# Relation sums from an always-one column and eight small DMAs, the 113-row transfers cut at a multiple of 16, and a later check of places, in a graph layer on one core

## What is computed

```python
h = maximum(layernorm(x), 0)
xs = h[src]
for r in range(4):
    w_r = where(edge_type == r, edge_weight, 0)
    total_msg += (xs @ W_rel[r] + b_rel[r]) * w_r[:, None]
agg = segment_sum(total_msg, dst) / maximum(segment_sum(edge_weight, dst), 1)[:, None]
x1  = layer_norm(h + h @ W_self + b_self + agg) * g1 + b1
ffn = gelu(x1 @ W_ffn1 + b_ffn1) @ W_ffn2 + b_ffn2
out = x + layer_norm(x1 + ffn) * g2 + b2
```

## Time and profile before

| | us |
|---|---|
| median of 3 runs (lowest, highest) | 349.38 (349.29, 350.85) |
| the profiled execution, its own time | 350.59 |
| its span, first to last instruction | 348.8 |
| busy: PE, PEld | 280.4, 250.1 |
| busy: DVE, ACT, POOL | 268.3, 144.9, 90.7 |
| mean granted TensorE clock | 0.949 |

### The profile page before, as it was taken

One profiled execution on the slowest core, in us unless ns is written; L12 is line 12 of the kernel. 1 busy time (PEld: TensorE's weight loads), 2 busy tenths in 40 slices (PEclk: granted clock), 3 DMA queues, 4 the chain that ended last, 5 costly groups with the idle time before them and its releaser, 6 DMA issues.

```text
span 348.8 us, 6519 instructions
## 1 busy us (share of the span) xinstructions
PE 280.4 (80%) x2602; PEld 250.1 (72%) x2602; DVE 268.3 (77%) x520; ACT 144.9 (42%) x180; POOL 90.7 (26%) x85
## 2 busy tenths in 40 slices
PE   2202965852999999999999999999999995999910
PEld 2201844642998899879997899879996895988810
DVE  4169999899979797979999798978434289796630
ACT  3033952735545456653745456553713224300000
POOL 3047392185000060001200040002100193493310
PEclk9999996995799999999999999999999998999985
DMA  5912114030000000000000000004006036001000
GB/s 164 265 28 59 63 26 155 2 121 3 2 0 2 3 3 2 2 1 2 2 3 2 0 3 2 3 0 166 18 2 210 31 106 181 14 0 60 30 34 23
DMA packets 8661, 15.62 MB, mean 45 GB/s; under 512 B 1667, under 2 KB 1887, under 8 KB 8630
## 3 DMA queue, kind: packets, MB, share of 16 engines
q1 hardware_dynamic: 8498, 15.03, 13.7%
q10 hardware_dynamic: 132, 0.17, 0.2%
HBM read 13.91 MB, written 1.28 MB: 44 GB/s over the span
## 4 chain that ended last, share of the span: by engine, by line
PE 54%; DVE 25%; issue 6%; DMA 4%; ACT 2%; POOL 2%; DVEq 2%; SPq 1%; POOLq 0%; ACTq 0%
PE psG L947 20%; PE psX L947 20%; PE psA L947 14%; DVE onehot L695 8%; DMA h<-in_x 4%; DVE wkey L697 3%; DVE keq L688 2%; DVE u_lo L924 2%; DVEq L624 1%; DVE u_hi L922 1%; ACT AT_hi L540 1%; POOL tbuf L343 1%; DVE A L713 1%; DVE small L752 1%; DVE tbuf L749 1%
## 5 line engine op out<-in xcount | busy, mean ns | idle before, releaser
L695 DVE TENSOR_SCALAR onehot<-iota_src,slot 125x640 f16<-125x640 f16 x200 | 77.1, 449 | 0.0
L947 PE MATMUL psA<-wkey,onehot 125*128 125x48 f16 (+5 forms) x1200 | 46.1, 196 | 18.0 <-DVE wkey L697 18.0
L947 PEld LDWEIGHTS psA<-wkey,onehot 125*128 125x128 f16 x1200 | 43.4, 99 | 21.9 <-DVE wkey L697 19.3
L505 ACT ACTIVATE away<-iota_src,slot 125x640 f16<-125x640 f16 x40 | 33.1, 827 | 40.4 <-PE psA L947 19.6
L947 PE MATMUL psG<-AT_hi,h_hi 128*128 128x256 f32 (+1 forms) x180 | 46.6, 295 | 0.4 <-ACT AT_hi L540 0.4
L947 PE MATMUL psG<-AT_hi,h_lo 128*128 128x256 f32 (+1 forms) x180 | 45.0, 286 | 0.0
L339 POOL TENSOR_SCALAR small<-small 128x1 f32<-128x1 f32 (+1 forms) x5 | 1.7, 333 | 165.3 <-DVE small L754 165.3
L947 PEld LDWEIGHTS psG<-AT_hi,h_hi 128*128 128x128 f32 (+1 forms) x180 | 34.8, 193 | 0.6 <-issue 0.5
L947 PEld LDWEIGHTS psG<-AT_hi,h_lo 128*128 128x128 f32 (+1 forms) x180 | 35.0, 194 | 0.0
L508 ACT ACTIVATE onehot<-away,ones_r 125x640 f16<-125x640 f16 x40 | 33.2, 829 | 1.3
L697 DVE TENSOR_TENSOR wkey<-keq,slot 125x624 f16<-125x624 f16 x40 | 32.9, 823 | 0.0
(11 more groups left out here) (154 smaller groups left out, 588.8 us busy)
## 6 DMA issues: line engine op xcount, KB each, us to landing
stage<-in_L_gnn_W_rel SPq DMA_DIRECT2D x8, 512.0 KB, 3.7
stage<-in_L_gnn_W_ffn SPq DMA_DIRECT2D x8, 512.0 KB, 4.1
h<-in_x SPq DMA_DIRECT2D x4, 256.0 KB, 4.2
stage<-in_L_gnn_W_self SPq DMA_DIRECT2D x2, 512.0 KB, 13.8
x_again<-in_x SPq DMA_DIRECT2D x4, 256.0 KB
out<-ybuf SPq DMA_DIRECT2D x4, 256.0 KB, 2.0
g_bc<-in_L_gnn_ln_g SPq DMA_DIRECT2D x2, 256.0 KB
b_bc<-in_L_gnn_ln_b SPq DMA_DIRECT2D x2, 256.0 KB
```

Of the source, the lines that this page charges most:

```text
L505: a.activation(away[0:EK, :], iota_src[0:EK, :], ACT.Abs, scale=-1.0, bias=slot[0:EK, b % SB, 0, SL - 1:SL]).then_inc(away_in, 1)
L695: v.tensor_scalar(oh[0:EK, j, :], iota_src[0:EK, :], f[:, 0, j:j + 1], None, ALU.is_equal)
L947: return nc.tensor.matmul(o, l, r, start=start, stop=stop, skip_group_check=True)
```

## The change

1. Transfers of a chunk of rows (load of x, second load of x, store of the result) are cut at a multiple of 16 rows: the chunk of 113 rows goes as 112 rows and 1 row.
2. The one-hot matrices are written 626 wide (OW), and column 626 holds a one for good. Row 114 of the last chunk of AT (SUMS) is then the column sum. `degrees` and evac_D are gone; SP moves that row of AT_hi and of AT_lo with 8 DMAs for each q (64 elements each, one relation to one partition) into D8 (8 x 128, two buffers), and b_rel is loaded twice, so that the bias product has 8 rows.
3. The check of places runs after the first build on DVE and after the first block on PE, and POOL takes the low part of W_self after the shift of the layer norm is out.

```diff
+    SPREAD = 16
+    SPANS = [[(0, m)] if m % SPREAD == 0 else [(0, m - m % SPREAD), (m - m % SPREAD, m)] for m in ROWS]
+    OW = N + 1
+    OS = OW + 1
+    SUMS = OS - 1 - (NT - 1) * P
...
             for c in range(NT):
-                sp.dma_start(h32[0:ROWS[c], c, :], x[c * P:c * P + ROWS[c], :]).then_inc(x_in[c], 16)
+                for p0, p1 in SPANS[c]:
+                    sp.dma_start(h32[p0:p1, c, :], x[c * P + p0:c * P + p1, :]).then_inc(x_in[c], 16)
+            def sums_by_relation(q):
+                if q >= 4:
+                    sp.wait_ge(W_ps, q // 2 - 1)
+                sp.wait_ge(AT_a, q + 1)
+                sp.wait_ge(AT_b, q + 1)
+                with nc.allow_non_contiguous_dma("one row to one partition by relation"):
+                    for part, half in enumerate((AT_hi, AT_lo)):
+                        row = f32(half[SUMS:SUMS + 1, q % 2, NT - 1, :]).rearrange("p (d r) -> p r d", r=R)
+                        for r in range(R):
+                            k = part * R + r
+                            sp.dma_start(D8[k:k + 1, q // 2 % 2, q % 2 * HD:(q % 2 + 1) * HD],
+                                         row[:, r, :]).then_inc(D_in[q % 2], 16)
+
             for u in range(NU):
+                if u == U_REL:
+                    for q in range(NQ - 2):
+                        sums_by_relation(q)
+                if u == U_REL + 2:
+                    for q in range(NQ - 2, NQ):
+                        sums_by_relation(q)
...
             g.tensor_tensor(rstd, var_e, mhalf, ALU.pow).then_inc(xrstd, 1)
+            pool.wait_ge(xnmr, 1)
             low_part(pool, 0)
...
-                    v.tensor_scalar(oh[0:EK, j, :], iota_src[0:EK, :], f[:, 0, j:j + 1], None, ALU.is_equal)
+                    v.tensor_scalar(oh[0:EK, j, 0:OW], iota_src[0:EK, 0:OW], f[:, 0, j:j + 1], None, ALU.is_equal)
...
-            def evac_D(q):
...
+            self_low(0)
+            low_part(dve, 1)
+            dve.wait_ge(iotas, 1)
+            dve.wait_ge(turned, 2)
+            pick(0, r[0])
+            build(0)
+            self_low(1)
 
             dve.wait_ge(first_in, 2)
...
-            self_low(0)
-            low_part(dve, 1)
-            dve.wait_ge(iotas, 1)
-            dve.wait_ge(turned, 2)
-            pick(0, r[0])
-            build(0)
...
-            def degrees(q):
...
             def rel_product(c):
 
                 m = ROWS[c]
-                pe.wait_ge(D_ev, 2 * c + 2)
-                mm(psX[0:m, :], D4[:, 0:m], brel_sb[:, :], True)
+                if c >= 1:
+                    pe.wait_ge(xT_b, c)
+                for i in range(2):
+                    pe.wait_ge(D_in[i], 16 * 2 * R * (c + 1))
+                mm(psX[0:m, :], D8[:, c % 2, 0:m], brel_sb[:, :], True)
...
-            pe.wait_ge(viol, 1)
-            pe.wait_ge(turned, 2)
-            mm(psA[:, NT - 1, 0:1], ones[0:EP, :], vsum, True, True).then_inc(vcnt, 1)
             self_product(0)
-            pe.wait_ge(regs_in, 1)
-            flag = pe.value_load(f_i32[0:1, NB:NB + 1], min_val=0, max_val=1 << 20)
             for i in range(HB):
                 build(0, range(i, i + 1))
+                if i == 0:
+                    pe.wait_ge(viol, 1)
+                    pe.wait_ge(hT_b, 2)
+                    mm(psG[:, 0, 0:1], ones[0:EP, :], vsum, True, True).then_inc(vcnt, 1)
+                    pe.wait_ge(regs_in, 1)
+                    flag = pe.value_load(f_i32[0:1, NB:NB + 1], min_val=0, max_val=1 << 20)
```

More of the change, by code:

```diff
@@ L40, in gnn_layer @@
     ROWS = [min(P, N - c * P) for c in range(NT)]
+    SPREAD = 16
+    SPANS = [[(0, m)] if m % SPREAD == 0 else [(0, m - m % SPREAD), (m - m % SPREAD, m)] for m in ROWS]
+    LOADED = [16 * len(spans) for spans in SPANS]
     EK = N // 5
@@ L63, in gnn_layer @@
     UC = 1024
+    OW = N + 1
+    OS = OW + 1
+    SUMS = OS - 1 - (NT - 1) * P
+    assert OW % 2 == 0 and OS <= NP
     EARLY = 3
@@ L217, in gnn_layer @@
         away_in = sem("away_in")
+        third = sem("third")
         keq_in = sem("keq_in")
@@ L228, in gnn_layer @@
         AT_b = sem("AT_b")
-        D_m = sem("D_m")
         G_ps = sem("G_ps")
@@ L232, in gnn_layer @@
         G_b = sem("G_b")
-        D_ps = sem("D_ps")
-        D_ev = sem("D_ev")
+        D_in = [sem(f"D_in{i}") for i in range(2)]
         deg_ps = sem("deg_ps")
@@ L370, in _ @@
                         sp.dma_start(buf[:, :], row.broadcast_to([P, D])).then_inc(consts_in, 16)
-                    sp.dma_start(brel_sb[:, :], b_rel).then_inc(consts_in, 16)
+                    for part in range(2):
+                        sp.dma_start(brel_sb[part * R:(part + 1) * R, :], b_rel).then_inc(consts_in, 16)
                     with nc.allow_non_contiguous_dma("bias by partition"):
@@ L381, in _ @@
             for c in range(NT):
-                sp.dma_start(x_again[0:ROWS[c], c, :], x[c * P:c * P + ROWS[c], :]).then_inc(late_in, 16)
+                for p0, p1 in SPANS[c]:
+                    sp.dma_start(x_again[p0:p1, c, :], x[c * P + p0:c * P + p1, :]).then_inc(late_in, 16)
             for buf, v in ((g2_bc, ln2_g), (b2_bc, ln2_b), (bf2_bc, b2)):
@@ L386, in _ @@
                 sp.wait_ge(y_out, c + 1)
-                sp.dma_start(out[c * P:c * P + ROWS[c], :], ybuf[0:ROWS[c], c % 2, :]).then_inc(out_done[c % 2], 16)
+                for p0, p1 in SPANS[c]:
+                    sp.dma_start(out[c * P + p0:c * P + p1, :], ybuf[p0:p1, c % 2, :]).then_inc(out_done[c % 2], 16)
             for i in range(2):
-                sp.wait_ge(out_done[i], 16 * len(range(i, NT, 2)))
+                sp.wait_ge(out_done[i], sum(LOADED[c] for c in range(i, NT, 2)))
         @block.gpsimd
@@ L440, in _ @@
                 low_part(pool, u)
-            pool.wait_ge(late_in, 16 * (NT + 3))
+            pool.wait_ge(late_in, sum(LOADED) + 16 * 3)
             for c in range(NT):
@@ L693, in build @@
                 oh, wk = ring(b)
+                if b == LATE + 2:
+                    v.memset(oh[0:EK, :, OW:NP], 0.0).then_inc(third, 1)
+                    dve.wait_ge(third, 1)
+                    v.memset(oh[0:EK, :, OS - 1:OS], 1.0)
                 for j in range(SL - 1):
-                    v.tensor_scalar(oh[0:EK, j, :], iota_src[0:EK, :], f[:, 0, j:j + 1], None, ALU.is_equal)
+                    v.tensor_scalar(oh[0:EK, j, 0:OW], iota_src[0:EK, 0:OW], f[:, 0, j:j + 1], None, ALU.is_equal)
                 dve.wait_ge(keq_in, b + 1)
@@ L1083, in rel_product @@
                 pe.wait_ge(G_b, 4 * c + 4)
-                mm(psG[0:m, 0, 0:1], D4[:, 0:m], ones[0:R, 0:1], True, True).then_inc(deg_ps, 1)
+                mm(psG[0:m, 0, 0:1], D8[:, c % 2, 0:m], ones[0:2 * R, 0:1], True, True).then_inc(deg_ps, 1)
                 for r in range(R):
```

29 lines of the change are left out of this document (13 added, 16 removed).

## The result

The changed kernel takes 332.27 us (median of 4 runs, 330.13 to 335.61) against 350.12 for the kernel before (4 runs, 349.29 to 351.39): the ratio is 0.947, interval 0.941 to 0.953. It is faster, as forecast, but by 18 us and not by 28, and it lies 2.3 us above the range. Medians and ranges in this document are of all runs, while the ratios leave out two (335.61 here and 353.81 of e3) that fell into a slower state of the chip.

What follows compares the result with a forecast made beforehand. The prediction took DVE to set the pace early and PE later. Start -9.8, four pairs -9.9, last pair +0.9 and end -8.9 summed to -27.7 us, from 349.38 to 322 us (rounded), range 316 to 330.

Steps and rivals of the forecast that it cites:

- the check of the eight DMAs: Steady pairs: issues 3.0 us plus landing 2.0, together 5.0, hidden in 7.75 us between AT_lo and the bias product.
- if rel_product waits for D8: Sign of being wrong: the bias product waits for the DMAs of the sums; the forecast expected no such wait.
- Four pairs, -9.9: Steady pairs: removing `degrees` takes 2.48 us a pair from PE, which is full there; four pairs give -9.9 us.
- Rival 3: Sums land late in the pairs: beyond 7.75 us each further us costs PE one us a pair; 328 or 367 us, chance 0.06.
- The last pair, +0.9: Last pair: the sums issued ahead of W_ffn1's third tile delay PE's early FFN product; gains nothing, loses 0.9 us.
- The start, -9.8: Start: fifth chunk's statistics 7.8 us earlier, layer norm's shift 2.0 us shorter, moved check 0; together -9.8 us.
- The end, -8.9: End: the last store, cut at 112 rows, takes 2.4 us against 11.3; -8.9 us.
- Rival 1: Start: W_self still lands late, so h starts 3.7 us earlier instead of 9.8; 328 us, chance 0.12.
- Rival 2: Order of the start or SP's queue (unit 12 late) costs 2 to 4 us more; 325 to 327 us, chance 0.15.
- Rival 5: More is gained, as the earlier check frees PE or unit 12 is hidden; 318 to 320 us, chance 0.08.
- Rival 4: DVE's one-hots of 626 columns lose their pace, 0.42 us more 200 times; 391 us, chance 0.04.

Runs made afterwards that it cites:

- e3: The kernel before with only the sums moved by DMA in place of the ones product: 350.37 us, ratio 0.999.
- e6: The changed kernel with the bias product behind the products of G high instead of ahead of them: 326.08 us, ratio 0.930.
- e7: The changed kernel with both e5's and e6's edits: 320.13 us, ratio 0.911.
- e8: The changed kernel with the four DMAs of AT_hi issued a second time, to rows that nothing reads: 348.95 us, ratio 0.994.
- e5: The changed kernel with unit 12 of the weights (third W_ffn1 tile) issued ahead of the last sums (q = 8 and 9): 324.76 us, ratio 0.924.
- e11: The changed kernel with each copy of sums reading 64 neighbouring elements in place of every fourth: 332.60 us, ratio 0.947.
- e1: The kernel before with only the transfers cut at 112 rows: 332.66 us, ratio 0.946.
- e2: The kernel before with only the later check of places and POOL's wait for the shift: 349.23 us, ratio 0.996.

## Why the prediction was wrong

**The step that failed** is the check of the eight DMAs: "Eight issues at 0.33 us, with 0.04 between them ... are 3.0 us". It was mis-sized: 0.59 us each, 5.0 us in all. I had taken the price of the small b_rel load from DRAM for a copy within the chip's buffer. The same number carried the last pair ("eight issues take until 254.7"). In the pairs the price alone would not have done it: 6.2 us still fit into 7.75, and into 6.7. The other side of the check was wrong too, with 6.7 us of room, and PE waited where a landing of 3.0 us came on top. The prediction's own sign of being wrong, "if rel_product waits for D8", came true.

- *Four pairs, -9.9.* Measured -4.4. The mechanism was right: without the late sums a pair is 36.50 us (e6, e7), the number forecast. Two sizes were off: the time to the last landing (6.2 us, 7.7 in pair 2, against 5.0), and the room (6.7 us against 7.75). I had read the 7.75 from the one pair in which POOL's product was stretched and not DVE's one-hots. The forecast also added the landing to the end of the last issue, where the trace counts it from its start; that erred to the safe side by one issue.
- *The price of a wait.* Rival 3 says that each further us costs PE one us. It costs more: a wait of 1.26 us was followed by 3.25 us at the lower clock. None of the five products of e7 had a wait for the sums, and each took 8.34 to 8.54 us; the four of e8 that took longer (10.16 to 11.76 us) each had one. I had priced waits as time alone. This was the larger part of what pair 2 lost. Short waits did not cost it: behind waits for the sums of 0.18, 0.46 and 0.52 us (e5, e3, e11) the same 34 matmuls took 8.57 to 8.59 us.
- *The last pair, +0.9.* Measured +5.0. From AT_lo's end (237.9 us) to the cast's end (247.7) it took 9.8 us, where I had 8.1: 2 us more of issues, 0.45 less of landing. A further 2.4 us came behind the wait, as above. e5 shows that none of it was necessary: the load only had to be issued first. Its last pair takes 35.3 us instead of 42.7.
- *The start, -9.8.* Measured -9.5, but by other parts than mine, so the agreement is luck. Two of them cancel: the shift did fall by 2.1 us, and the order of the check, which I took as 0 with an end at +2, gave that back. The check itself takes DVE 8.8 us (26.79 to 35.58) where it took 7.2 in the kernel before (25.88 to 33.04), and the first build, now beside POOL's 7.44 us from 16.76, is stretched too: its keys take 1.50 us instead of 0.48, its slots 1.25 instead of 0.17. The fifth statistics alone brought more than my 7.8: POOL's scale starts 1.16 us behind the statistics in e1, 2.64 in the kernel before. That extra is not certain: in e7, which has the cut, it is 2.63 again, and the first AT_lo stands at 60.7 us. Its cause stays open.
- *The end, -8.9.* Measured -9.4.

**The rivals.** Rival 1 (W_self late) fell: it landed in a median of 6.4 us instead of 13.8 and was converted 1.2 us before ACT needed the shift. So it had indeed stood behind the 113-row load: with the cut alone (e1) the median is 6.0 us, with the check alone (e2) 13.5. Rival 2 came true in one of its halves, unit 12, and in the other, the check, only so far that it took back the shift's gain. Rival 3 came true, but in one pair of the five, and there with a price beyond the wait. I had priced each of them alone, at 325 to 328; both hang on the same issue price, and together, with the clock, they make 332. That is why the range was too narrow at the top. Rival 5 (more is gained) did not come true. Rival 4 fell: five one-hots of 626 columns take 1.55 us, of 640 took 1.56. DVE, kernel after:
```profile
126.04 1.55 DVE L731 TENSOR_SCALAR onehot<-iota_src,slot 125x626 f16<-125x626 f16 x5
```
Both rules of the Trainium skill that I cited held. That of DMA: Bandwidth & Descriptors, "Why a DMA increments its semaphore by 16 and not by 1", was about the 113 rows: with 112 and 1 rows SP waits 1.5 us for the last store where with 113 it waited 11.1, and e1, which has this cut alone, gains as much as the whole change. That of Vector Engine (DVE) Microarchitecture Reference, 5.1, asks for an even count, which 626 is, and the pace of 626 columns bears it out.

**What stays open.** What sets 0.59 us for the issue of a one-row copy within the buffer, while one-row loads of x from DRAM cost 0.29, was not found; e11 excludes the stride alone. The time of an issue is not fixed by its kind either: the load of 1024 elements that held SP for 1.18 us in the earlier trace rows took 0.40 in the changed kernel, and the two b_rel loads there 0.37 and 0.46 instead of the 0.33 of the one. Why the landing of q = 5 is slow in every kernel is open, and so is what decides which of DVE and POOL is stretched. That the wait brings the lower clock rests on e6, e7 and e8: without the wait there is no slow product, and behind each of the four waits of e8 there is one.

## What to carry to other kernels

Price the issue of a small DMA from a row of the same kind (source memory and shape), look at more than one pair for the room that it has, and multiply: eight issues in a row are a delay of their own, also for whatever large load stands behind them on that queue. Put a wait that may come late where PE still has other work ahead of it, since here PE lost 1.6 to 3.3 us on top of each wait of 1.26 us and more for the sums or for W_hi. And look for transfers with a row count such as 113, which no number from 2 to 16 divides: here they held some 17 of the 31 us that were gained in the end (e1 and e7).

## What the runs showed that I had not expected

- A copy of 64 elements from one partition to another holds SP for 0.59 us at issue, strided or not, and mostly lands 1.8 us after issue. The slowest copy takes 3.0 to 4.9 in the groups q = 5 and q = 8 of every kernel.
- A PE wait of 1.26 us, in a stretch in which PE was otherwise busy, was followed by about 7 us of mostly the lower clock level (0.57 granted from 170 to 178 us), and cost 3.25 us in addition. A wait of 5.0 us cost 2.4 more, in e6 1.6.
- Where five one-hots of DVE meet a product of POOL (128 x 512, float32), either DVE takes 3.65 us instead of 1.57 or POOL 2.91 instead of 1.28.
- One-hots of 626 columns, two halves of 313, keep the pace of 640.
- A DVE operation on 5 elements takes 2.25 us beside POOL's two-input product and 0.17 us without it (e2 shows the same: `22.31 0.17 DVE L674`).
